# Four result buffers, results sent by halves, and a regrouped last stage in a two-layer recurrent and expert kernel

## The reference

```python
P = jax.nn.softmax(x @ Wg, axis=-1)          # 8 experts
_, topk_idx = jax.lax.top_k(P, 2)            # each token goes to two of them
P_norm = P * mask / ((P * mask).sum(-1, keepdims=True) + EPS)
h   = jax.nn.gelu(einsum('bsd,edf->ebsf', x, W1) + b1, approximate=False)   # F = 512
y_e = einsum('ebsf,efd->ebsd', h, W2) + b2
g   = einsum('ebsd,bse->bsd', y_e, P_norm)
x   = x + s * silu(g)
```

## Time and profile before

| | us |
|---|---|
| median of three runs (lowest, highest) | 453.9 (452.7, 454.86) |
| the profiled execution | 452.68 |
| its span, first to last instruction | 450.9 |
| PE busy | 413.2 (92%) |
| PE weight loads | 346.0 (77%) |
| DVE busy | 285.3 (63%) |
| ACT busy | 213.9 (47%) |
| POOL busy | 155.6 (35%) |

### The profile page before, as it was taken

One profiled execution on the slowest core, in us unless ns is written; L12 is line 12 of the kernel. 1 busy time (PEld: TensorE's weight loads), 2 busy tenths in 40 slices (PEclk: granted clock), 3 DMA queues, 4 the chain that ended last, 5 costly groups with the idle time before them and its releaser, 6 DMA issues.

```text
span 450.9 us, 9851 instructions
## 1 busy us (share of the span) xinstructions
PE 413.2 (92%) x2944; PEld 346.0 (77%) x2944; DVE 285.3 (63%) x1137; ACT 213.9 (47%) x525; POOL 155.6 (35%) x215
## 2 busy tenths in 40 slices
PE   7699998999999999999988999888999999999863
PEld 6579777878869779787767879687998999898521
DVE  4869888888888878878867666422344344333217
ACT  3364646565554545543423434334555555555212
POOL 6440015013232340343333012454454555554400
PEclk9989999999999999999999999999999999999988
DMA  7459511253164330132213123412222222222656
GB/s 182 117 117 150 68 39 34 58 155 122 37 186 120 81 85 21 46 82 52 77 51 77 47 51 90 118 55 65 73 70 60 72 71 71 70 71 66 233 189 189
DMA packets 64211, 40.80 MB, mean 90 GB/s; under 512 B 18341, under 2 KB 57129, under 8 KB 64169
## 3 DMA queue, kind: packets, MB, share of 16 engines
q1 hardware_dynamic: 59472, 31.27, 28.8%
q0 software_dynamic: 4352, 8.99, 6.0%
q10 hardware_dynamic: 344, 0.03, 0.1%
HBM read 21.78 MB, written 18.48 MB: 89 GB/s over the span
## 4 chain that ended last, share of the span: by engine, by line
PE 44%; issue 19%; DVE 15%; DMA 8%; SPq 6%; ACT 5%; POOL 1%; DVEq 1%; POOLq 0%; ACTq 0%
PE psB L855 6%; PE psA L1029 5%; PE psB L843 5%; PE psC L1041 3%; DMA ring<-routed 2%; DMA results<-nat,y_to 2%; PE psB L1052 2%; PE psD L972 2%; DMA routed<-send,slot 2%; SPq L490 1%; DVE stats L1325 1%; PE psD L957 1%; PE psC L746 1%; PE psB L845 1%; POOL routed L694 1%
## 5 line engine op out<-in xcount | busy, mean ns | idle before, releaser
L694 POOL DMA_INDIRECT routed<-send,slot x64 | 64.3, 1004 | 129.0 <-DMA routed<-send,slot 59.8
L707 POOL DMA_INDIRECT results<-nat,y_to x72 | 70.1, 974 | 91.8 <-DVE nat L1638 36.5
L1029 PE MATMUL psA<-xuT,w_all 128*128 128x256 f32 x288 | 69.1, 382 | 2.7 <-ACT h1T L1239 2.1
L1239 ACT ACTIVATE h1T<-psA,b1T 128x256 f32<-128x256 f32 x144 | 63.2, 474 | 12.0 <-PE psB L1052 7.8
L1029 PEld LDWEIGHTS psA<-xuT,w_all 128*128 128x128 f32 x288 | 50.5, 190 | 10.8 <-ACT h1T L1239 2.6
L1610 DVE TENSOR_SCALAR xu<-ring 128x256 f32 (+1 forms) x38 | 11.3, 297 | 74.9 <-DMA ring<-routed 65.2
L1041 PE MATMUL psC<-w_all,h1T 128*128 128x128 f32 x464 | 56.9, 276 | 1.0 <-DVE nat L1622 1.0
L1041 PEld LDWEIGHTS psC<-w_all,h1T 128*128 128x128 f32 x464 | 54.1, 192 | 1.7 <-ACT h1T L1239 1.1
L1230 ACT ACTIVATE xuT<-psB 128x256 f32<-128x256 f32 x37 | 14.2, 383 | 62.4 <-PE psB L1019 43.0
L843 PE MATMUL psB<-xnT,w_l 128*128 128x512 f32 x64 | 34.9, 627 | 0.0
L1170 ACT ACTIVATE hg0T<-psB,b1T 128x512 f32<-128x512 f32 x32 | 22.0, 688 | 23.6 <-PE psB L845 23.5
(11 more groups left out here) (289 smaller groups left out, 853.8 us busy)
## 6 DMA issues: line engine op xcount, KB each, us to landing
ring<-routed SPq DMA_DIRECT2D x38, 130.0 KB
inv<-inv_room SPq DMA_DIRECT2D x8, 512.0 KB, 4.2
w_all<-results SPq DMA_DIRECT2D x15, 256.0 KB, 4.7
routed<-ring SPq DMA_DIRECT2D x24, 130.0 KB, 7.7
n_room<-nT SPq DMA_DIRECT2D x8, 256.0 KB
w_all<-in_L_ffn_W_dram SPq DMA_DIRECT2D x1, 2048.0 KB
out_dram<-x_all SPq DMA_DIRECT2D x8, 256.0 KB, 2.3
results<-nat,y_to POOLq DMA_INDIRECT x72
```

Of the source, the lines that this page charges most:

```text
L694: pool.indirect_dma_start(routed[:, :], bass.IndirectOffsetOnAxis(ap=slot[par][:, c, t:t + 1], axis=0), send[par][:, c, t, :], None).then_ ...
L707: pool.indirect_dma_start(results[:, :], bass.IndirectOffsetOnAxis(ap=y_to[:, par, a:a + 1], axis=0), yw[:, par, a, :], None).then_inc(S[f ...
L1029: last = mm(psA[:, j // 2, (j % 2) * UNIT:(j % 2 + 1) * UNIT], w1_all[:, e, j * P:(j + 1) * P], xuT[:, :], start=True, stop=True)
L1239: f(h1T[:, j, :], psA[:, j // 2, (j % 2) * UNIT:(j % 2 + 1) * UNIT], ACT.Gelu, bias=b1T[:, n:n + 1]).then_inc(S["gelu_ready"], 1)
```

## The change

- `YBUFS` = 4 result buffers `yw` in place of 2, each with its own semaphore `y_sent0` to `y_sent3`; `yb` gets its own memory. DVE waits for the landing of unit u-4 in place of u-2.
- DVE's `results_of` takes place and weight first (and so raises `ring_free`), then multiplies b2 by the weight (two operations of 128 values, from SBUF), and only then waits for PE's product, half by half, and makes `psum * weight + yb` in one operation for each half. PE raises `out_ps` when the first half is done; in the first eight units, whose halves share a bank, DVE waits for both. `yw_ready` counts halves.
- POOL sends a half as soon as it is ready, and waits for the landing of the unit before after both. Its loop has four units in a round; up to three surplus units fill the last round. Their sends go to spare rows.
- The last unit's out is done half by half on PE. Ahead of it PE adds the first group's lower half (`between`, `lower(0)`).
- SP has no surplus loads; it raises `unit_in` by their amount instead.
- The last stage: silu goes to the memory of the W1 weights, so ACT waits for no buffer. DVE takes groups (0), (1,2), (3,4), (5,6), (7); for groups 3 and 4 it only multiplies, PE adds x_all and the product with the identity, and ACT copies the sum to x_all. SP stores in the order 0, 1, 2, 5, 6, 3, 4, 7.

```diff
+ENDS = ((0, 1), (1, 3), (3, 5), (5, 7), (7, 8))
+ENDS_PE = (3, 4)
+STORES = (0, 1, 2, 5, 6, 3, 4, 7)
+YBUFS = 4
...
+        def mix1(first, end):
+            return w1_all[:, first:end, :].rearrange("p g (t d) -> p (g t) d", d=D)
...
     (other_units)
+            between()
             out(bounds[E] - 1, E - 1, None)
...
     (SP)
-            load_unit(bounds[E], 0)
-            load_unit(bounds[E] + 1, 0)
-            wait_on(sp, "unit_in", (bounds[E] + 2) * 16)
+            wait_on(sp, "unit_in", bounds[E] * 16)
             sp.sem_inc(apart, 1)
+            sp.sem_inc(S["unit_in"], 2 * 16)
...
-            for g in range(groups):
-                sp.wait_ge(S["x2_ready"], g + 1)
+            by_dve = 0
+            for g in STORES:
+                if g in ENDS_PE:
+                    sp.wait_ge(S["x3_ready"], ENDS_PE.index(g) + 1)
+                else:
+                    by_dve += 1
+                    sp.wait_ge(S["x2_ready"], by_dve)
...
     (POOL)
-            def send_results(u, par):
-                wait_on(pool, "yw_ready", u + 1)
-                pool.sem_inc(apart, 1)
+            def send_results(u, buf):
                 for a in range(HALVES):
-                    if a and not (isinstance(u, int) and u == 0):
-                        pool.wait_ge(S[f"y_sent{1 - par}"], (u + par) * (8 * HALVES))
-                        pool.sem_inc(S["y_landed"], 1)
+                    wait_on(pool, "yw_ready", u * HALVES + a + 1)
+                    pool.sem_inc(apart, 1)
                     pool.indirect_dma_start(...)
+                if not (isinstance(u, int) and u == 0):
+                    pool.wait_ge(S[f"y_sent{(buf - 1) % YBUFS}"], ...)
+                    pool.sem_inc(S["y_landed"], 1)
...
     (PE)
-                wait_on(pe, "yb_ready", u)
+                wait_on(pe, "yw_ready", u * HALVES)
...
-            other_units(pe, bounds, hid, out)
-            for g in range(groups):
+            def lower(g):
                 pe.wait_ge(lower_in[g], 16)
...
+            other_units(pe, bounds, hid, out, lambda: lower(0))
+            for g in range(1, groups):
+                lower(g)
...
+            for n, g in enumerate(ENDS_PE):
+                pe.wait_ge(S["silu1_ready"], n + 1)
+                mm(sum_ps_of(n), ident[:, :], x_all[:, g * TILES:(g + 1) * TILES, :], start=True, stop=False)
+            for n, g in enumerate(ENDS_PE):
+                pe.wait_ge(S["mix_ready"], g + 1)
+                mm(sum_ps_of(n), ident[:, :], w1_all[:, g, :], start=False, stop=True).then_inc(S["x3_ps"], 1)
...
     (DVE)
+                wait_on(dve, "yw_ready", u * HALVES)
+                wait_on(dve, "y_landed", u - YBUFS + 1)
...
+                for a in range(HALVES):
+                    last = v.tensor_scalar(yb[:, a, :], b2_all[:, f, :], y_wt[:, a:a + 1], None, ALU.mult)
+                last.then_inc(S["yb_ready"], 1)
                 wait_on(dve, "yb_ready", u + 1)
                 for a in range(HALVES):
-                    last = v.tensor_scalar(yw[:, mine, a, :], yb[:, a:a + 1, :], y_wt[:, a:a + 1],
-                                           None, ALU.mult)
-                last.then_inc(S["yw_ready"], 1)
+                    if a == 0 and not one_bank:
+                        wait_on(dve, "out_ps", u + 1)
+                    else:
+                        wait_on(dve, "h1_free", (u + 1) * JF)
+                    v.scalar_tensor_tensor(yw[:, mine, a, :], ps[:, a:a + 1, :], y_wt[:, a:a + 1], yb[:, a:a + 1, :],
+                                           ALU.mult, ALU.add).then_inc(S["yw_ready"], 1)
```

More of the change, by code:

```diff
@@ L437, in unit_bounds, with other_units @@
                     for e in range(first, last)]
-        def other_units(eng, bounds, hid, out):
+        def other_units(eng, bounds, hid, out, between=lambda: None):
             for e in range(E):
@@ L1035, in out @@
             def out(u, f, e):
-                wait_on(pe, "yb_ready", u)
+                wait_on(pe, "yw_ready", u * HALVES)
+                if e is None:
+                    for a in range(HALVES):
+                        for k in range(JF):
+                            if a == 0:
+                                wait_on(pe, "gelu_ready", u * JF + k + 1)
+                            last = mm(psC[:, a, 0:D], h1T[:, k, a * P:(a + 1) * P],
+                                      w2_all[:, f * JF + k, :], start=(k == 0), stop=(k == JF - 1))
+                            if a == HALVES - 1:
+                                last.then_inc(S["h1_free"], 1)
+                        if a == 0:
+                            last.then_inc(S["out_ps"], 1)
+                    return
                 for k in range(JF):
@@ L1656, in _, with finish @@
             other_units(dve, bounds, lambda u, e: take_ahead(u), lambda u, f, e: results_of(u, f, psC[:, :, 0:D]))
-            wait_on(dve, "yw_ready", bounds[E])
-            dve.sem_inc(S["yw_ready"], 1)
-            def finish(g):
-                ts = slice(g * TILES, (g + 1) * TILES)
-                m = mix2[g % 2][:, :, :]
-                dve.wait_ge(S["silu1_ready"], g + 1)
-                v.tensor_tensor(m, s1[:, ts, :], th1[g % 2][:, :, :], ALU.mult).then_inc(S["mix_ready"], 1)
-                dve.wait_ge(S["mix_ready"], g + 1)
-                v.tensor_tensor(x_all[:, ts, :], x_all[:, ts, :], m, ALU.add).then_inc(S["x2_ready"], 1)
+            wait_on(dve, "yw_ready", bounds[E] * HALVES)
+            for n in range(YBUFS - 1):
+                wait_on(dve, "y_landed", bounds[E] + n - YBUFS + 1)
+                mine = bass.ds((bounds[E] + n) % YBUFS, 1)
+                v.tensor_scalar(y_to[:, mine, :].rearrange("p r a -> p (r a)").unsqueeze(2),
+                                spare[:, mine, :].rearrange("p r a -> p (r a)").unsqueeze(2), 0.0, None,
+                                ALU.add).then_inc(S["yw_ready"], HALVES)
+            def finish(first, end):
+                ts = slice(first * TILES, end * TILES)
+                m = mix1(first, end)
+                dve.wait_ge(S["silu1_ready"], end)
+                v.tensor_tensor(m, s1[:, ts, :], m, ALU.mult).then_inc(S["mix_ready"], end - first)
+                if first not in ENDS_PE:
+                    dve.wait_ge(S["mix_ready"], end)
+                    v.tensor_tensor(x_all[:, ts, :], x_all[:, ts, :], m, ALU.add).then_inc(S["x2_ready"], end - first)
             dve.wait_ge(S["s1_ready"], groups)
-            for g in range(groups):
-                finish(g)
+            for first, end in ENDS:
+                finish(first, end)
 _INS = ['L0_attn_x', 'L0_attn_W_qkv', 'L0_attn_W_out', 'L0_attn_b_out', 'L0_ffn_gate_w', 'L0_ffn_w1',
```

77 lines of the change are left out of this document (39 added, 38 removed).

## The result

The changed kernel takes 460.1 us (median of 4 runs, 459.7 to 461.2) beside 453.3 for the kernel before (4 runs): ratio 1.017, 95% interval 1.013 to 1.021. It is 1.7% slower; the forecast was 448.4 us and faster. The profiled execution has a span of 457.4 us against 450.9.

A forecast was written before the change was run, and what follows sets the result against it. PE was taken to bound the loops, and after 419.5 us a chain of sends, loads and DVE's last stage. Terms -4.5 (parts 1 to 3), -1.0, -1.9, +1.9 sum to -5.5: 452.68 to 447.2, plus 1.2 gives 448.4 us; range 445.0 to 452.0.

The forecast's parts named there:

- Part 1: Loops of the units: earlier ring_free shortens the load circle and DVE gets ahead of PE; -0.7 us, between 0 and -1.7.
- DVE's work for a unit grows ... so nothing: Loops: DVE's added 0.2 to 0.6 us in a unit costs nothing, beside 41.76 busy us of 109.5.
- Rival (c): Loops: unit loads collide with back-to-back sends, a unit takes 4.2 us, total 458 us, slower; chance 0.06.
- Part 2: Start of the first results load: at 417.95, 1.5 us earlier, without the surplus loads.
- Part 3: Last unit: sends 1.27 us apart, second-half loads earlier; -4.5 us with Part 1 and Part 2, far end -2.1.
- the near end: Last send's landing: 2.23 us after its start, at 427.3, as with idle DMA engines; far end 4.61 us, 429.7.
- Then the PE wait of part 3 costs nothing: Ahead of the last out: PE's 2.15 us wait is free, since earlier sends would only take longer among loads.
- Part 4: PE's clock before the last stage: stays full, first silu 1.0 us after the data; -1.0 us, between 0 and -1.1.
- Rival (b): PE's clock falls in the 2.15 us wait ahead of the last out; 451.0 to 453.0, say 451.5 us; chance 0.09.
- Part 5: DVE's last stage: nine operations take 9.2 us in place of 11.1; -1.9 us.
- Part 6: Final stores: five within 2.1 us queue up, giving back +1.9 us.
- rival (d): End: stores or PE's sums for two groups come last and eat Part 5 whole; 450.3 us, chance 0.10.

The follow-up runs named there:

- e10: Changed kernel with an extra VectorE sum (1.2 us) ahead of POOL's sends, only in the loops' units: 451.6 us, 0.998 to the kernel before.
- e6: Changed kernel with VectorE's old order, POOL's old wait between sends, and both halves waited for ahead of the first send: 449.5 us, 0.998.
- e11: e10 with the delaying sum cut to 512 values (some 0.6 us expected): 469.6 us, 1.043 to the kernel before.
- e12: e10 with the delaying sum cut to 128 values (some 0.2 us expected): 466.9 us, 1.037 to the kernel before.
- e5: Changed kernel with POOL's sends of every unit held for an extra VectorE sum over 1024 values: 454.8 us, 1.011 to the kernel before.
- e8: e6 with the old last stage (VectorE one group at a time, no PE additions, stores in order): 0.996 to the kernel before.
- e13: e10 with the first group's addition behind the last out and the old last stage: 447.0 us, 0.993 to the kernel before.
- e9: e6 with the first group's addition behind the last unit's out, not ahead of it: 0.999 to the kernel before.
- e7: Kernel before the change, with VectorE signalling and POOL sending each half of a unit's results once ready: 449.7 us, 1.001.

## Why the prediction was wrong

**Part 1 failed.** It has -0.7 us for the loops; they cost some 11 us more. The step that failed is "DVE's work for a unit grows ... so nothing", with the four buffers counted as a wait gone: each edit was priced by its engine's time, and what it does to the start of POOL's sends was put at nothing. What the edits changed was when POOL sends. In the kernel before, VectorE had its results later and the landing of the unit before held sends back (24.7 us of waiting); the last send near an out's end started 0.45 us behind that end in the median. With VectorE's products done as soon as PE's are, four buffers and signals by halves, VectorE alone releases them,

```profile
L719 POOL DMA_INDIRECT results<-nat,y_to x48 | 48.2, 1003 | 54.1 <-DVE nat L1684 45.3 <-issue 8.9
```

and the second send starts 1.39 us ahead of the end of out, so that out's last signals fall into the 0.2 to 1.4 us after it in which PE's signals come late. That cost 0.4 us in the mean of 27 units (4.23 for 3.82), some 11 us; the first results load came 10 us later than forecast (427.96 for 417.95). e10 shows that the start of the sends is the cause: PE's code is the same and VectorE's has only a sum more, the sends are later, and the loops are at 3.73 in the median. e6 shows it without any added work, and e11 and e12 show that added work at the wrong length makes it worse. Rival (c) named the sends being back to back, but by another mechanism, loads that collide with them. The loads were not late, and with pairs still 1.27 us apart the loops of e5 and e10 are fast. That (c) named a unit of 4.2 us and a time of 458 us, close to the 4.23 and 460.1 measured, is luck.

The Trainium skill, "DMA: Bandwidth & Descriptors", section SWDGE vs HWDGE vs iDMA, says that POOL's descriptors are state in SBUF which VectorE's two-port mode locks POOL out of. If VectorE's new operations on SBUF run in that mode, which no row tells, they could have been the cause, by longer sends. In the loops a send took 1003 ns in the mean against 976 before, and in e10, with yet more of VectorE's work, 969: not here.

**Part 2** held as a mechanism: the surplus loads no longer stand ahead of the first results load. Its time went with the loops, and one term was mis-sized: the signal that unit 32 has landed was to come 0.9 us behind the start of unit 33's second send. The load started at 427.96, 0.5 us behind the start of the first send (427.44) and 0.75 ahead of the second (428.71).

**Part 3** was right on the sends (1.27 us apart, landing 2.24 us later, where 2.23 was forecast at the near end) and on the segment, -2.6 of the -3.0 expected. It was right for the wrong reason: PE waited 0.64 us ahead of the last addition and not 2.15. The load started 2.0 us behind the end of unit 33's product (425.96) and not 3.25, because of the signal just named, and unit 34's out was 0.3 us later than forecast. In the kernels whose loops are fast the wait is there, 2.0 to 2.35 us in e5, e6, e8 and e10, and costs: 2.1 us between e10 and e13. "Then the PE wait of part 3 costs nothing" failed. With the wait between the sends (e9) a landing hides a part of it: 1.0 us came back.

**Part 4** held in the changed kernel. The clock stayed full and the first silu came 3.79 us after the loads' start (437.75 to 441.54) against 4.63 before: -0.84 for -1.0. In e13 and e8, where PE stands idle longer, the half clock of the earlier trace rows is back. Rival (b), the clock falling ahead of the last out, did not come here, where PE waited 0.64 us, but came in e6, e8 and e10.

**Part 5** was mis-sized. The stage of compute, first silu to last result, is 11.1 us in the new kernel against 11.7, -0.6 and not -1.9: operations of 1.22 to 1.23 us are as estimated, but loads landed until 446.6, VectorE waited for silus, and PE's additions and ACT's copy ended last. **Part 6** was right in kind and size: 4.7 us from the last copy to the span's end against 2.7, +2.0 for +1.9. Together they are a loss of 1.4 us. That is rival (d). e8, with the old stage, is not slower than e6, and takes 18.9 us from the second half's loads to the end where e6 takes 20.5; e13 takes 18.7.

## What to carry to other kernels

A wait that seems to cost little may be what keeps two engines' events apart. When buffers are added, ask what releases the next work now, and at what point of the critical engine's cycle it falls; look in the trace for units that are already slower and for what fell together there. Shift the suspect by a known time in both directions before believing a cause, and measure where the edge is. And move an addition ahead of the last unit only if its data are there: the last unit is on the path, the addition is not.

## What the runs showed of the hardware

With two indirect sends by POOL 1.27 us apart, signals for PE's products that end from about 0.2 to 1.4 us after the second's start come late: of 399 of PE's signals recorded late (over 0.06 us behind the product's end), 394 stand 0.7 to 0.9 or 1.4 to 1.7 us after that start. PE's work itself isn't longer; only who waits for it is late, up to 1.2 us for gelu. ACT's signals to PE were on time in 195 of 200 such waits, and for VectorE's nothing is shown: the expectations of the runs name all three engines, and the traces bear out PE alone. Many records of ACT's and VectorE's signals are missing in that stretch. The table's edge at -0.2 to -0.4 us (the end of out just ahead of that time) and its slow fall from 4.69 to 3.89 us as the send moves away both fit one stretch of late signals. It isn't exact: e7 has fast units at -0.35, and e10 one of 4.54 us at 0.07, with three sends in a row, 1.5 and 1.27 us apart. What in a send causes it, descriptors being written, packets starting or completions, was not tried and stays open; so does whether a kernel with a second buffer for gelu's output, whose circle would be open, is free of it.

TensorE's clock: with waits of 2.00, 2.31 and 2.35 us ahead of the last unit's addition (e10, e8, e6) the granted clock fell to 0.50, 1.2 GHz, in the addition or in the out behind it. With waits of 0.57 to 1.99 us at the same place (nine kernels) it stayed at 2.4 GHz there. The 1.99 us of e5 and the 2.00 of e10 differ in outcome, so the length of this wait doesn't tell it alone.
